# Twelve-layer decoder on one core: set-up joined to the main program, projections of the 32-head stage moved ahead of the scores, last layer's ternary weight made early, its norms rearranged

## What is computed

```
x = _layernorm(x + _L0_attn_ref(x, ...))     # retention, 8 heads
x = _layernorm(x + _L0_xattn_ref(x, ctx_1024, ...))
x = _layernorm(x + _L0_ffn_ref(x, ...))      # mixture of 8 experts, top 2
...                                          # layers 1 and 2
x = _layernorm(x + _L3_attn_ref(x, ...))     # 32 heads of 32, output norm
x = _layernorm(x + _L3_xattn_ref(x, ctx_1024, ctx_1024, ...))
x = _layernorm(x + _L3_ffn_ref(x, L3_ffn_weight, L3_ffn_gamma, L3_ffn_beta))
```

```
xn = (x - mu) * rsqrt(var + EPS) * gamma + beta
scale = max(max(abs(xn)), 1e-8) / 127;  xq = round(clip(xn / scale, -127, 127)) * scale
delta = 0.7 * mean(abs(w));  mask = abs(w) > delta
alpha = sum(abs(w) * mask) / max(sum(mask), 1);  wq = alpha * sign(w) * mask
return einsum('bsi,oi->bso', xq, wq)
```

## Time and profile before

| what | us |
|---|---|
| median of 3 timed runs | 1448.85 |
| lowest and highest of them | 1442.31, 1449.97 |
| profiled execution, all of it | 1460.55 |
| profiled execution, first to last instruction | 1458.7 |
| TensorE busy | 1230.4 |
| VectorE busy | 918.5 |
| ScalarE busy | 649.7 |
| GpSimd busy | 170.3 |

### The profile page before, as it was taken

One profiled execution on the slowest core, in us unless ns is written; L12 is line 12 of the kernel. 1 busy time (PEld: TensorE's weight loads), 2 busy tenths in 40 slices (PEclk: granted clock), 3 DMA queues, 4 the chain that ended last, 5 costly groups with the idle time before them and its releaser, 6 DMA issues.

```text
span 1458.7 us, 27476 instructions
## 1 busy us (share of the span) xinstructions
PE 1230.4 (84%) x10752; PEld 858.3 (59%) x10752; DVE 918.5 (63%) x2432; ACT 649.7 (45%) x1253; POOL 170.3 (12%) x242
## 2 busy tenths in 40 slices
PE   2489999999999999997888998787879986898751
PEld 1356766776676767775555676454556564556530
DVE  2463453536786878877775877975875446544557
ACT  2134345445544554456543446442436643554320
POOL 3221021102200200020000120000030001000011
PEclk9589999999999999998997999997989999999975
DMA  7001110111021102110000010000000000000000
GB/s 273 1 1 44 44 30 17 57 51 52 10 64 51 52 1 73 30 30 1 2 1 1 2 37 1 1 2 1 2 1 2 1 2 2 1 2 1 2 0 29
DMA packets 23143, 35.59 MB, mean 24 GB/s; under 512 B 4568, under 2 KB 12904, under 8 KB 22760
## 3 DMA queue, kind: packets, MB, share of 16 engines
q1 hardware_dynamic: 23016, 33.83, 7.5%
HBM read 32.77 MB, written 1.05 MB: 23 GB/s over the span
## 4 chain that ended last, share of the span: by engine, by line
PE 70%; DVE 13%; ACT 8%; issue 6%; POOL 1%; DVEq 0%; ACTq 0%; POOLq 0%
PE banks L1187 12%; PE banks L1171 11%; PE banks L1925 5%; PE banks L1938 4%; PE banks L1946 3%; DVE arena L2066 2%; ACT XALL L535 2%; PE banks L1967 2%; PE banks L923 2%; PE banks L897 2%; PE banks L545 2%; PE banks L1920 2%; PE banks L661 2%; PE banks L1886 1%; PE banks L937 1%
## 5 line engine op out<-in xcount | busy, mean ns | idle before, releaser
L2066 DVE TENSOR_REDUCE arena<-banks 128x4 f32<-128x1024 f32 x128 | 151.1, 1219 | 106.1 <-PE banks L1902 106.0
L1187 PEld LDWEIGHTS banks<-WE,arena 128*128 128x128 f32 x1536 | 180.0, 192 | 24.4 <-issue 23.3
L1231 ACT ACTIVATE arena<-banks,BC 128x512 f32<-128x512 f32 x192 | 130.5, 688 | 120.2 <-PE banks L1171 119.9
L1187 PE MATMUL banks<-WE,arena 128*128 128x128 f32 x1536 | 182.3, 276 | 0.0
L1171 PE MATMUL banks<-XT,WE 128*128 128x512 f32 x384 | 179.0, 602 | 0.0
L2044 ACT ACTIVATE arena<-banks 128x1024 f32<-128x1024 f32 x128 | 126.4, 1022 | 112.2 <-PE banks L1925 111.5
L1271 DVE SCALAR_TENSOR_TENSOR R<-banks,arena,R 128x128 f32<-128x128 f32 x256 | 71.9, 343 | 111.2 <-PE banks L1187 110.9
L1925 PE MATMUL banks<-arena 32*128 32x256 f32 x1024 | 112.7, 396 | 0.0
L579 ACT COPY arena<-banks 128x512 f32<-128x512 f32 x108 | 61.3, 591 | 115.2 <-PE banks L574 35.8
L1171 PEld LDWEIGHTS banks<-XT,WE 128*128 128x128 f32 x384 | 69.2, 192 | 69.1 <-issue 67.6
L1741 DVE TENSOR_TENSOR arena<-arena 128x512 f32<-128x512 f32 x144 | 100.8, 700 | 3.8
(11 more groups left out here) (305 smaller groups left out, 2149.4 us busy)
## 6 DMA issues: line engine op xcount, KB each, us to landing
WE<-in_weights SPq DMA_DIRECT2D x64, 256.0 KB, 2.9
WE<-in_weights SPq DMA_DIRECT2D x64, 128.0 KB, 2.2
WS<-in_weights SPq DMA_DIRECT2D x1, 2368.0 KB, 13.2
RW<-in_rows SPq DMA_DIRECT2D x1, 1032.0 KB
XALL<-in_x SPq DMA_DIRECT2D x4, 256.0 KB, 10.8
out_dram<-arena SPq DMA_DIRECT2D x4, 256.0 KB, 2.3
WS<-in_weights SPq DMA_DIRECT2D x1, 900.0 KB, 7.9
WS<-in_weights SPq DMA_DIRECT2D x1, 645.0 KB, 8.0
```

The costliest lines, as they stand in the source:

```text
L1187: ins = PE.matmul(v[:, tile(t)], self.HT[:, e % 2, j, tile(t)], self.W[:, (8 * i + e) % RING, 1, j], start=j == 0, stop=j == self.J - 1)
L1231: A.activation(self.HT[:, e % 2, j], psum.view(f"{self.L}.h{i}.{e}.{j}"), ACT.Relu, bias=bcol(self.p + "_b1", e * self.J + j))\
L2066: V.tensor_reduce(big.mx[:, 2 * pair:2 * pair + 2], v, AX.X, ALU.max, negate=True).then_inc(dve.read(f"big.m{i}.{n}.{pair}"), 1)
```

## The change

**Set-up in one program.** The set-up's parts become functions (`setup_sp`, `setup_pool`, `setup_act`, `setup_dve`), which the engines run at the head of the main block. TensorE begins with a wait for 23 steps of GpSimd's set-up (the identity in both types), VectorE waits for the whole decay table before the first product with it, GpSimd for VectorE's masks. The first weight group is loaded in two DMAs: 4 x 128 columns, which the first projections read, and the rest, which counts as one of the small loads.

**32-head stage.** The projection of turn n+2 stands between the maxima and the scores of turn n, where the projection of turn n+3 stood behind the value sums; ScalarE's copies of it stand ahead of the exponentials.

**Ternary weight.** It is made in `x0` of chunk 0, in three pieces on VectorE (after its second maxima, two slots later, and after its output), with two all-reduces on GpSimd.

**Last norms.** The second norm of `x3` has mean 0 and its variance follows from the first, so both powers come from one set of statistics, and y is computed from R. The apply to XALL stands behind the maxima. The very last norm is applied by ScalarE, except for half of the last chunk, which VectorE does.

```diff
@@ set-up
-        with nc.Block(no_gpsimd_drain=True) as block:
-            @block.sync
-            def _(sp):
+        def setup_sp(sp):
...
-                load_group(sp, 0)
+            sp.dma_start(WS[:, 0:4 * D], weights[:, 0:4 * D]).then_inc(w_loaded[0], 16)
+            sp.dma_start(WS[:, 4 * D:GROUP_AT[1]], weights[:, 4 * D:GROUP_AT[1]]).then_inc(small_loaded, 16)
...
@@ ret_dve
+                    if i == 0 and k == 0:
+                        dve.eng.wait_ge(setup_step, 31)
...
+        tern, tern_neg, tern_w = (R[:, CHUNKS - 1, k] for k in range(3))
+        def tern_rows_dve(dve):
+            dve.eng.wait_ge(w_loaded[6], 16)
+            V.tensor_reduce(tern_row, W("L3_ffn_weight"), AX.X, ALU.add, apply_absolute_value=True)\
+                .then_inc(dve.flag("tern.rows"), 1)
+        def tern_parts_dve(dve):
+            w = W("L3_ffn_weight")
+            dve.eng.wait_ge(sig("tern.total"), 1)
+            V.tensor_scalar(tern_delta, tern_total, 1.0 / (D * D), 0.7, ALU.mult, ALU.mult).then_inc(dve.step(), 1)
...
+            V.tensor_scalar(tern, w, tern_delta, None, ALU.is_gt).then_inc(dve.step(), 1)
...
+            V.tensor_copy(tern16[:], tern).then_inc(dve.flag("tern.w16"), 1)
...
+            V.tensor_reduce(tern_row_sums[:, 0:1], tern_w, AX.X, ALU.add).then_inc(dve.flag("tern.parts"), 1)
+        def tern_scale_dve(dve):
+            dve.eng.wait_ge(sig("tern.totals"), 1)
...
@@ Cross.dve
                 self.maxima_dve(dve, i, 1)
-                yield
-                yield
+                if L == "x0" and i == 0:
+                    tern_rows_dve(dve)
+                yield
+                yield
+                if L == "x0" and i == 0:
+                    tern_parts_dve(dve)
...
                     end_sum_dve(dve, L, i, f"{L}.o.out", "xb")
+                    V.tensor_scalar(rstd_fin[:, tiles_of(i)], mv[:, tiles_of(i), 1], 1.0 + EPS, EPS * EPS, ALU.mult, ALU.add)\
+                        .then_inc(dve.flag("fin.var"), 1)
                     yield
-                    norm_apply(dve, i, R[:, i], xc(i), L)
-                    norm_stats(dve, i, xc(i), "fin", EPS)
-                    yield
-                    y = R[:, i]
-                    norm_apply(dve, i, xc(i), y, "fin")
+                    y = XB[:, slot(i)]
+                    dve.eng.wait_ge(sig("fin.rstd"), i + 1)
+                    for t in range(4):
+                        k = 4 * i + t
+                        V.tensor_scalar(y[:, t], R[:, i, t], mv[:, k, 0:1], rstd_fin[:, k:k + 1],
+                                        ALU.subtract, ALU.mult).then_inc(dve.step(), 1)
...
                     V.tensor_reduce(ABSMAX[:, tiles_of(i)], y, AX.X, ALU.max,
                                     apply_absolute_value=True).then_inc(dve.step(), 1)
+                    norm_apply(dve, i, R[:, i], xc(i), L)
@@ Cross.pool
+                    G.partition_all_reduce(tern_total, tern_row, P, bass.bass_isa.ReduceOp.add)\
+                        .then_inc(pool.flag("tern.total"), 1)
...
@@ big_pe
-            project(2)
             shifts(0)
             yield
             for n in range(GROUPS + 1):
                 if n + 1 < GROUPS:
                     maxima(n + 1)
+                if n + 2 < GROUPS:
+                    project(n + 2)
                 if n < GROUPS:
                     scores(n)
...
-                if n + 3 < GROUPS:
-                    project(n + 3)
@@ big_act
+                if n + 2 < GROUPS:
+                    copies(n + 2)
                 if n < GROUPS:
                     for pair in range(2):
...
-                if n + 3 < GROUPS:
-                    copies(n + 3)
@@ last_pool, last_dve, last_act
             for c in range(CHUNKS):
+                norm_mean(pool, c, "last")
                 norm_rstd(pool, c, "last")
+                norm_shift(pool, c, "last")
...
-            for c in range(CHUNKS):
-                norm_apply(dve, c, last.RR[:, c], last.OUT[:, c], "last", "last.out")
+            c = CHUNKS - 1
+            dve.eng.wait_ge(sig("last.rstd"), c + 1)
+            for t in range(2):
...
+            for c in range(CHUNKS):
+                act.eng.wait_ge(sig("last.offset"), c + 1)
+                for t in range(4 if c < CHUNKS - 1 else 2):
...
+                    ins = A.activation(last.OUT[:, c, t], last.RR[:, c, t], ACT.Identity, bias=shift[:, k:k + 1],
+                                       scale=rstd[:, k:k + 1])
@@ main block
             @block.tensor
             def _(eng):
+                eng.wait_ge(setup_step, 23)
                 run(0, lambda i: eng)
```

More of the change, by code:

```diff
@@ L1010, in dve @@
                 yield
+                if L == "x0" and i == 0:
+                    tern_scale_dve(dve)
                 yield
@@ L2034, in big_act @@
             yield
-            copies(2)
             shift_copy(0)
@@ L2249, in last_dve @@
                 norm_stats(dve, c, last.RR[:, c], "last", EPS)
[L2250 to L2251 removed]
+            c = CHUNKS - 1
+            dve.eng.wait_ge(sig("last.rstd"), c + 1)
+            for t in range(2):
+                k = 4 * c + t
+                ins = V.tensor_scalar(last.OUT[:, c, t], last.RR[:, c, t], mv[:, k, 0:1], rstd[:, k:k + 1],
+                                      ALU.subtract, ALU.mult)
+                if t:
+                    ins.then_inc(dve.flag("last.half"), 1)
+                else:
+                    ins.then_inc(dve.step(), 1)
         def last_act(act):
@@ L2296, in _ @@
                 for c in range(CHUNKS):
+                    if c == CHUNKS - 1:
+                        sp.wait_ge(sig("last.half"), 1)
                     sp.wait_ge(sig("last.out"), c + 1)
```

283 lines of the change are left out of this document (148 added, 135 removed).

## The result

| | before | changed |
|---|---|---|
| median of the executions timed together, us | 1448.57 (6) | 1432.29 (6) |
| lowest and highest | 1442.31, 1460.64 | 1429.23, 1435.48 |
| ratio, 95% interval | | 0.9879 [0.9839, 0.9920] |
| a second measurement: medians | 1453.12 (11) | 1431.55 (6) |
| its ratio | | 0.9852 [0.9822, 0.9883] |

The kernel became 16 to 22 us faster, where 34.5 were predicted: 1432 against 1414, and outside the range. (One execution of the later kernel pmvs, the profiled one, took 2361.55 us; it is left out of every number, and nothing is read from its trace.) The two profiled executions differ by 30.7 us, nearly what was predicted from a profile. So two things are to be explained: which parts gave less, and why profiles and medians differ.

A forecast was written before the change was run, and what follows sets the result against it. TensorE, busy 84%, was taken to set the pace, leaving the ends and the 32-head stage's waits. 15.2 + 5.9 + 1.5 + 14 - 2.1 = 34.5 us off 1448.85 gave 1414, range 1396 to 1430.

The forecast's parts named there:

- Start: Set-up: first matmul near 7.45 us instead of 22.64, gaining 15.2 us; ends about 7 and 15.2.
- half lost: Rival at the start: TensorE's slow clock level lasts longer, 7 of the 15 us go: 1422 us; chance 0.10.
- My own condition: Sign of being wrong: the middle stages between 50 and 700 us do not keep their length.
- Ternary form: First cross attention: VectorE's added pieces, partly hidden by a 0.60 us wait, lose 2.1 us; ends 0 and 3.0.
- GpSimd's own order: First cross attention: two all-reduces precede chunk 1's gate product, not due for several slots; costs nothing.
- End: Last chunk's tail: 5.9 us gained up to the quantisation and 1.5 us after it.
- Order of the 32-head stage: Projection between maxima and scores: a turn 6.15 us instead of 6.44, 19 over 64 turns, 14 us taken.
- waits change places only: Rival in the 32-head stage: TensorE stays behind VectorE's reduction, without the 14 us: 1428; chance 0.18.
- the rival of an unmoved start: Rival at the start: a wait for first weights or a later landing replaces the barrier: 1429; chance 0.03.
- Base: Starting time for the subtraction: 1448.85 us, median of the shown runs, 11.7 below the profiled execution's 1460.55.

The follow-up runs named there:

- pmvs: Changed kernel with 32-head-stage turns ordered projection, maxima, value sums, scores; ScalarE's copies as in values_first: mean 1408.6 us, ratio to the kernel before 0.9678.
- before_again: The kernel before, unchanged, measured against itself: mean 1455.9 us, ratio 1.0020.
- start_only: The kernel before with only the set-up in one program: mean 1443.5 us, ratio to before 0.9923.
- after_again: The changed kernel, unchanged, measured again: mean 1432.5 us, ratio to the kernel before 0.9852.
- warm_start: Changed kernel plus 40 products nobody reads, on TensorE in its waits between 18 and 54 us: mean 1430.9 us, ratio to the kernel before 0.9831.
- ends_only: The kernel before with only the early ternary form and the changed last norms: mean 1454.4 us, ratio to before 1.0006.
- tern_moe0: Changed kernel with the ternary form made in chunk 0's first expert stage, not its cross attention: mean 1430.4 us, ratio to the kernel before 0.9838.
- copy_first: Changed kernel with ScalarE's copy of the value sums ahead of its shift copy in each 32-head-stage turn: mean 1439.2 us, ratio to the kernel before 0.9905.
- both: Changed kernel with the edits of tern_moe0 and copy_first, plus an unread all-reduce in chunk 3's last cross attention: mean 1433.7 us, ratio to the kernel before 0.9867.
- old_order: Changed kernel with the old order of the 32-head stage: mean 1436.6 us, ratio to the kernel before 0.9873.
- order_only: The kernel before with only the new order of the 32-head stage: mean 1453.7 us, ratio to before 0.9998.
- values_first: Changed kernel with value sums of turn n-1 ahead of the scores of turn n, their ScalarE copy ahead of the exponentials: mean 1429.3 us, ratio to before 0.9823.

## Why the prediction was wrong

**Start.** Right in the chain: 7.45 and 13.73 us, no wait for a weight, 15.1 us ahead at 69 us. In executions it gave 9.6 (mean) to 11.4 (median) against before, and 12.4 against the mean of before_again; the clock's part took the rest. In start_only's trace 1.7 us of it are the longer stretch at the lower level at the start (34.1 instead of 30.7 us, at half the speed). I can't place more: it lies in short stretches at that level, and these differ between executions of one kernel as well: changed kernel and after_again, the same program, are 16.5 and 11.8 us ahead of before at 470 us. The rival "half lost" put some 8 us on this part, which fits the executions about as well, but its mechanism is wrong: warm_start shows that the slow level at the start itself costs some 1.5 us. My own condition, that 50 to 700 us keep their length, failed: the changed kernel is 15.1 us ahead of before at 69 us, 9.7 at 142 and 17.0 at 674.

**Ternary form.** Mis-sized, 3.0 to 3.7 instead of 2.1. VectorE's nine operations are as long as summed (75.06 to 77.18 = 2.1 us) and the reciprocal behind them comes 1.5 us later, as said (5.49 us after the start of the long one, before 3.95); but until the variance all but 0.5 of it is absorbed by waits that stood there anyway, so this term was too large. The step that failed is "GpSimd's own order gets the two all-reduces ahead of chunk 1's gate product, which is not due for several slots: nothing". The gate product was due at 75.14, and it comes 7.10 us after the second all-reduce, with chunk 0's norm behind it, 2.0 us late. That idle time could not be seen before, since all three all-reduces stood at the end with nothing after them for long; the 5.62 before them in the earlier trace rows could.

**End.** 7.4 predicted; 7.5 gained in ends_only, 5.2 in the changed kernel. The two stretches themselves took 7.84 and 5.4 us, as forecast (7.8 and 5.4); the other 2 us went ahead of them: from the last transposed x to the last residual sum it took 24.7 us before and 26.8 now, with the granted clock at 0.69 instead of 0.77. It needs the new order and the other parts together: after_again, tern_moe0, copy_first, both and warm_start have 26.8 there as well, old_order 24.7 and order_only 25.3. That the all-reduce comes some 2 us behind its operand (2.46) was right by chance: it is bound to GpSimd's last power, 6 us before. An apply on ScalarE took 0.48 us in the tail, as the estimate from the Trainium skill (ScalarE: Activation LUTs, What ACT_TABLE_LOAD costs) had it, 479 ns; nobody waited for the twelve. (One sum of the prediction there is wrong: 1.7 us more would have made 1416, not 1417.)

**Order of the 32-head stage.** The term that failed most: 14 predicted, 3.4 alone and 6.4 beside the others in the full-clock part, 0 to 4 in executions. The turn itself was right, 6.18 against 6.15, with the wait of 0.46 for ScalarE and VectorE's reduction as its bound. The step that failed is the multiplication, "Over 64 turns that is 19", of which I took 14 for what the mixed turns might do. Only 18 of the 63 intervals between two turns' maxima in the trace have that length, which is worth 18 times 0.27 = 5 us; in mixed turns the waits changed places (20.5 us for VectorE instead of 8.2), in chunk 1's stretch the lead was given back, in chunk 3's the clock took it. The rival "waits change places only" (1428) has the mechanism that the traces show and came near; in number the rival of an unmoved start (1429) is as near, and the start did move. What the stage had to give was there: filling VectorE's 2.35 us with the value sums and putting the projection ahead of the maxima gave 24 us more than the changed order. The value sums alone gave nothing in the full-clock part; the projection alone ahead of the maxima was not tried.

**Base.** I subtracted from 1448.85, the median of three executions; the later measurements gave 1451.98 to 1456.41, so some 4 of the 18 us of error are the base. That the profiled execution's 12 us were the clock's was not seen. The 1426 worked out against that execution are 4 us off the changed kernel's profile by luck. The terms were 9 too large in the full-clock part (34.5 against 25.2 by the means), but these two executions lie some 29 us apart in it, 4 more than the means, and their clock's parts are alike within 2 us, where the mean of the changed kernel's is 4 larger.

What stays open: why the clock's part differs between kernels (112.3 in copy_first, 102.0 in values_first), how the three parts help each other, and how much of what the ternary form costs at the start is the clock's.

## What to carry to other kernels

When a turn of a pipelined loop is too long, write down the chain that closes it (here maxima, VectorE's reduction, second scores) and put independent work of the right length into that gap; moving work that already fits changes who is waited for. For a small gain a turn, count only the turns that run alone; for mixed ones, take nothing without a row. And where executions spread, compare span times granted clock beside the medians: it told 3 us apart where medians could not. It misleads where a change moves the clock in a stretch that waits for other engines: in warm_start it rose by 12.8 us, and the kernel was no slower.

## What the runs showed of the hardware

GpSimd stands idle 5.5 to 6.1 us between its last other operation and a first all-reduce, whether the operand is there or not, and 7.1 us between the last all-reduce and the next other operation (6.6 to 7.7 in seven traces, always at the same place). A second one right behind the first has neither. Both are put down to "issue", so no wait in the profile names them; the trace has a MODIFY_POOL_CONFIG at the head of each.

TensorE's mean granted clock differs between executions of the same program (0.925 to 0.936), and with it the time, by 16 us in 1450. Less waiting did not bring more clock: in chunk 3's stretch of order_only TensorE was idle for 4.9 us less and was granted 0.93 instead of 0.96. Nor did more clock always bring time: in warm_start it was 0.96 instead of 0.57 from 20 to 60 us, and chunk 0's chain there was 1.2 us ahead.
